# Eight phases of routed FFN with a moving-average attention: state adds on VectorE in the last phase, its last job in halves, gathers spread, attention batches moved forward, weight loads ahead of broadcasts on SyncE's queue

## The reference, cut to what matters

```python
xn = _layernorm(x)
# branch 1: per feature a causal convolution whose kernel is a sum of two decaying
# exponentials (an exponential moving average), plus xn * omega, then silu
out = irfft(rfft(xt, n=2*S) * rfft(k, n=2*S))[..., :S]
attn = silu(transpose(out) + xn * omega)
# branch 2: four rounds of a mixture of 4 experts, two of them for each token
for r in range(4):
    vals, idx = top_k(flat @ Wg[r] + bg[r], 2)
    cw = sum(one_hot(idx, 4) * softmax(vals)[..., None], axis=1)
    hmid = gelu(einsum('nh,ehf->enf', flat, W1) + b1[:, None, :])   # 128 -> 512
    y = einsum('enf,efh->enh', hmid, W2) + b2[:, None, :]           # 512 -> 128
    cur = cur + einsum('ne,enh->nh', cw, y)
x = x + attn + cur
```

## Time and profile before

| | |
|---|---|
| median of 3 runs | 706.83 us (705.14 to 710.83) |
| the profiled execution | 702.66 us |
| its span, first to last instruction | 700.8 us |
| mean granted TensorE clock | 0.961 |
| busy share of TensorE, its weight loads, VectorE, ScalarE, GpSimd | 88%, 73%, 68%, 74%, 59% |
| DMA, mean over the span | 208 GB/s |

### The profile page before, as it was taken

How to read it: one execution, slowest core, us unless ns; L and a number is a source line. 1 busy time by engine, 2 the same in 40 slices (tenths; PEclk the granted TensorE clock), 3 DMA queues, 4 the chain that set the end, 5 groups by cost and what they waited for, 6 DMA issues and landing times.

```text
span 700.8 us, 11414 instructions
## 1 busy us (share of the span) xinstructions
PE 616.5 (88%) x3289; PEld 508.3 (73%) x3289; DVE 473.7 (68%) x1049; ACT 515.9 (74%) x979; POOL 412.4 (59%) x432
## 2 busy tenths in 40 slices
PE   7667999999998998999989989998999898888580
PEld 6455877888787887888778877887788776677360
DVE  4963786688864885578656876587758875795350
ACT  4668778898786877788877877886788686777550
POOL 5658438552874375536843584438568785855664
PEclk9999999999999998999999999999899999999995
DMA  8011012646886587667975689568767798658510
GB/s 240 10 55 48 15 55 87 212 165 219 310 256 254 204 304 250 224 227 253 329 268 198 250 282 283 222 218 289 238 241 251 270 307 271 237 197 305 191 60 30
DMA packets 85898, 145.92 MB, mean 208 GB/s; under 512 B 21911, under 2 KB 49486, under 8 KB 85838
## 3 DMA queue, kind: packets, MB, share of 16 engines
q1 hardware_dynamic: 79540, 133.06, 54.8%
q0 software_dynamic: 5824, 11.87, 5.3%
q10 hardware_dynamic: 474, 0.28, 0.1%
HBM read 37.42 MB, written 12.09 MB: 71 GB/s over the span
## 4 chain that ended last, share of the span: by engine, by line
PE 50%; DVE 12%; POOL 10%; issue 9%; DMA 8%; ACT 5%; SPq 3%; another core or an unknown queue 1%; POOLq 1%; DVEq 1%; ACTq 0%
PE z L1383 8%; PE y L1399 8%; PE y L1401 7%; PE z L1385 7%; PE y L1400 7%; PE z L1384 7%; PE spare L1308 4%; POOL sorted_rows L754 4%; DVE h_lo L1216 3%; DMA w_job<-w_all 3%; POOL state L740 3%; DMA sorted_rows<-rows,position_i 3%; ACT z L889 2%; ACT h_hi L892 2%; PE misc L1330 2%
## 5 line engine op out<-in xcount | busy, mean ns | idle before, releaser
L1216 DVE TENSOR_TENSOR h_lo<-z,h_hi 128x512 fp32r<-128x512 f32 (+1 forms) x428 | 251.6, 597 | 132.6 <-ACT h_hi L892 99.1
L889 ACT ACTIVATE z<-z,b_job 128x512 f32<-128x512 f32 (+1 forms) x364 | 212.2, 583 | 102.9 <-PE z L1385 76.5
L892 ACT CAST h_hi<-z 128x512 fp32r<-128x512 f32 (+1 forms) x428 | 221.4, 517 | 13.5
L740 POOL TENSOR_TENSOR state<-state,weighted 128x512 f32<-128x512 f32 (+1 forms) x103 | 115.6, 1122 | 130.0 <-DVE weighted L1163 128.1
L1399 PE MATMUL y<-h_hi,w_job 128*128 128x512 f32 (+1 forms) x364 | 134.7, 370 | 22.6 <-DVE h_lo L1216 13.8
L1383 PE MATMUL z<-cur_hi,w_job 128*128 128x512 f32 (+1 forms) x364 | 139.3, 383 | 13.4 <-DMA w_job<-w_all 10.3
L754 POOL DMA_INDIRECT sorted_rows<-rows,position_i x112 | 118.2, 1055 | 32.6 <-issue 22.4
L1400 PE MATMUL y<-h_lo,w_job 128*128 128x512 f32 (+1 forms) x364 | 130.1, 357 | 0.0
L1401 PE MATMUL y<-h_hi,w_job 128*128 128x512 f32 (+1 forms) x364 | 129.9, 357 | 0.0
L1384 PE MATMUL z<-cur_lo,w_job 128*128 128x512 f32 (+1 forms) x364 | 129.8, 357 | 0.0
L1385 PE MATMUL z<-cur_hi,w_job 128*128 128x512 f32 (+1 forms) x364 | 129.4, 356 | 0.0
(11 more groups left out here) (164 smaller groups left out, 791.9 us busy)
## 6 DMA issues: line engine op xcount, KB each, us to landing
w_job<-w_all SPq DMA_DIRECT2D x182, 512.0 KB
gate_bc<-gate_rows SPq DMA_DIRECT2D x72, 256.0 KB
rows<-sorted_rows SPq DMA_DIRECT2D x28, 266.0 KB, 3.7
gate_bc<-gate_rows SPq DMA_DIRECT2D x35, 128.0 KB
out_dram<-x_tok SPq DMA_DIRECT2D x8, 256.0 KB, 5.5
sorted_rows<-rows,position_i POOLq DMA_INDIRECT x112
b_job<-b_all SPq DMA_DIRECT2D x91, 2.5 KB
rows<-in_L_ffn_W_dram SPq DMA_DIRECT2D x4, 256.0 KB, 7.5
```

The lines of the kernel that those rows point to most:

```text
L740: pool.tensor_tensor(state[job.g][:, cols_at], before, weighted[:, j % TR, 0:job.n], ALU.add).then_inc(added, 1)
L889: nc.scalar.activation(zs, zs, ACT.Gelu_apprx_tanh, bias=bias).then_inc(gelu_done, 1)
L892: nc.scalar.copy(h_hi[:, s % ZR, 0:job.n], zs).then_inc(hi_act, 1)
L1216: dve.tensor_tensor(h_lo[:, s % ZR, 0:job.n], zs, hs.bitcast(F32), ALU.subtract).then_inc(lo_done, 1)
```

## The change

**1. State adds of the last phase on VectorE.** `add_last(j)` stands right behind `combine(j)` on VectorE and replaces GpSimd's `add(j)` in phase 7. It counts up a semaphore of its own, `added_last`, on which the transpositions of that phase wait.

**2. The last job in halves.** F7 of phase 7 becomes H0 and H1 of 256 tokens with the same expert, weights being loaded for each. The transposition, addition and finish of the last block fall in two halves, called "Q", of two tiles each.

**3. Gathers and step numbers.** The gathers of phase 7 move from the steps 23 to 40 to the steps 6 to 37, those of phase 6 one or two steps ahead; several P steps of both phases move by up to 6.

**4. Attention.** EMA_PHASE changes from (1, 2, 3, 4, 5, 6, 7, 7) to (1, 1, 2, 2, 3, 4, 5, 6): the phases 1 and 2 work two batches each (the second at the steps 0 to 14), phase 7 none.

**5. SyncE's queue.** For a job it was W1, W2, bias of the same job, gate broadcast of the job before. Now it is W1, W2, and then bias and gate broadcast of the job behind it. W1 of a phase's first job is issued before `load_sorted` waits. `b_job` has 6 slots. Each of the four DMAs reads the table itself, so there are four TENSOR_LOADs for a job instead of two.

**6. Small moves.** P split 49 to 48, jobs 31 to 30, two scatters one step later.

```diff
-LAST_JOBS = "F0 F1 F2 F3 X0 X1 X2 X3 X4 F4 F5 F6 F7".split()
+LAST_JOBS = "F0 F1 F2 F3 X0 X1 X2 X3 X4 F4 F5 F6 H0 H1".split()
...
 SORTED = {
-    "P": (42, 44, 51, 53), "P copy": (46, 48, 53, 57), "P split": (44, 46, 49, 55),
+    "P": (42, 44, 51, 53), "P copy": (46, 48, 53, 57), "P split": (44, 46, 48, 55),
...
-    "places": (17, 18), "pairs": (22, 22), "order": 22, "pick": 27, "jobs": 31, "table": 35,
-    "scatter": (19, 20, 20, 20, 21, 23, 24, 24, 25, 27, 31, 33, 35, 35, 40, 42), "load": 45}
+    "places": (17, 18), "pairs": (22, 22), "order": 22, "pick": 27, "jobs": 30, "table": 35,
+    "scatter": (19, 20, 20, 20, 21, 23, 24, 24, 25, 27, 31, 33, 35, 36, 41, 42), "ema 2": (0, 1, 2, 3, 4, 6),
+    "ema tanh 2": 6, "A 2": 10, "A add 2": 14}
...
 LAST_PHASE = {
-    "P": (40, 41, 49, 58), "P add": (43, 44, 51, 61), "finish": (47, 45, 52, 63),
-    "ema": ((-3, 1, 2, 3, 4, 7), (9, 11, 12, 14, 15, 19)), "ema tanh": (5, 19), "A": (6, 19), "A add": (8, 22),
-    "idents": 26, "gather": (23, 25, 26, 27, 28, 28, 28, 30, 35, 35, 35, 36, 38, 38, 39, 40)}
+    "P": (38, 41, 47), "P add": (41, 43, 50), "finish": (41, 46, 53), "idents": 4,
+    "gather": (6, 9, 11, 11, 12, 12, 16, 17, 19, 22, 24, 26, 30, 31, 33, 37), "Q": (56, 56), "Q add": (57, 58),
+    "Q finish": (57, 58)}
 BEFORE_LAST = {
-    "P add": (43, 46, 53, 57), "finish": (48, 50, 54, 58), "idents": -1,
-    "gather": (1, 1, 2, 2, 3, 3, 4, 4, 6, 6, 6, 6, 7, 7, 11, 11)}
-EMA_PHASE = (1, 2, 3, 4, 5, 6, LAST, LAST)
+    "P add": (43, 46, 51, 53), "finish": (48, 51, 54, 57), "idents": -3,
+    "gather": (-1, 1, 2, 2, 3, 3, 3, 4, 4, 4, 4, 5, 8, 9, 11, 12)}
+EMA_PHASE = (1, 1, 2, 2, 3, 4, 5, 6)
...
-            for j in range(NJ + 1):
-                if DENSE <= j < NJ:
-                    job_weights(j)
-                if j > 0:
-                    job = JOBS[j - 1]
-                    if job.kind == "D" and job.e == 0:
+            for j, job in enumerate(JOBS):
+                if job.kind == "D":
+                    if job.e == 0:
                         gates_out(("G", 0, job.b))
-                    if job.kind == "F" and job.i == 0:
-                        gates_out(("G", job.p, 0))
+                    broadcast_gate(j)
+                    continue
+                last_of_phase = j + 1 == NJ or JOBS[j + 1].p > job.p
...
+                if job.turn == 0:
+                    sp.wait_ge(table_ready, 3 * job.p)
+                    job_bias(j)
+                job_w1(j)
+                if job.turn == 0:
+                    load_sorted(job.p)
+                job_w2(j)
+                if not last_of_phase:
+                    job_bias(j + 1)
+                if job.turn == 1:
+                    gates_out(("G", job.p, 0))
                     broadcast_gate(j - 1)
-                for p in SORT_GATE:
-                    if j == LOAD_AT[p] // FC + 1:
-                        load_sorted(p)
+                    broadcast_gate(j)
+                if job.turn > 0 and not last_of_phase:
+                    broadcast_gate(j + 1)
                 for b in range(B):
-                    if j == T_AT["A", b] // FC + 3:
+                    if j == ADD_AT["A", b] // FC + 3:
                         store_x(b)
...
+            def add_last(j):
+
+                job = JOBS[j]
+                if job.kind == "X":
+                    if job.i == 0:
+                        dve.wait_ge(table_ready, 3 * LAST)
+                    dve.reg_load(half_at, table_i[LAST % 2][0:1, 13 + job.i:14 + job.i])
+                    cols_at = bass.ds(dve.snap(half_at, min_val=0, max_val=GT - HALF), HALF)
+                else:
+                    cols_at = job_cols(job)
+                dve.wait_ge(combined, j + 1)
+                wait(dve, added_last, j - FIRST[LAST])
+                dve.tensor_tensor(state[1][:, cols_at], state[1][:, cols_at], weighted[:, j % TR, 0:job.n],
+                                  ALU.add).then_inc(added_last, 1)
```

More of the change, by code:

```diff
@@ L31 @@
 WR = 3
+BR = 6
 GR = 4
@@ L66, in job_list @@
             for turn, name in enumerate(LAST_JOBS if p == LAST else SORTED_JOBS):
-                full, i = name[0] == "F", int(name[1])
-                jobs.append(Job(p, g, name[0], i, i // 2 if full else None, None, BLK if full else HALF, turn))
+                kind, i = name[0], int(name[1])
+                b = {"F": i // 2, "X": None, "H": NB - 1}[kind]
+                jobs.append(Job(p, g, kind, i, b, None, BLK if kind == "F" else HALF, turn))
     return jobs, first
@@ L86, in block_done, with last_half_done, add_on_dve @@
     return 1 + max(j for j, job in enumerate(JOBS) if job.p == p and (job.kind == "X" or job.b == b))
+def last_half_done(half):
+    done = [j for j, job in enumerate(JOBS) if job.p == LAST and (job.kind == "X" or job.b == NB - 1)]
+    return 1 + max(j for j in done if JOBS[j].kind != "H" or JOBS[j].i == half) - FIRST[LAST]
+def add_on_dve(j):
+    return JOBS[j].p == LAST
 def hi_on_dve(s):
@@ L452, in wait, with job_cols @@
                 eng.wait_ge(s, value)
+        def job_cols(job):
+            first = job.b * BLK + (job.i * HALF if job.kind == "H" else 0)
+            return slice(first, first + job.n)
         def block_cols(b):
@@ L566, in broadcast_gate @@
                     start = from_table(job.p, 23 + job.i, ZERO_GATE - BLK)
+                elif job.kind == "H":
+                    start = from_table(job.p, 23 + 2 * NB - 1, ZERO_GATE - BLK) + job.i * HALF
                 else:
@@ L774, in _ @@
                 for j in range(max(s // FC - 3, 0), s // FC + 1):
-                    if combine_at(j) + 1 == s:
+                    if combine_at(j) + 1 == s and not add_on_dve(j):
                         add(j)
@@ L798, in _ @@
                             gather(p, t)
-                    for b in range(NB):
-                        if FINISH_AT[p, b] == s:
-                            finish(p, b)
-            add(NJ - 1)
-            for b in range(NB):
-                if FINISH_AT[LAST, b] >= STEPS:
-                    finish(LAST, b)
+                for name, when in FINISH_AT.items():
+                    if when == s:
+                        finish(name)
+            for name, when in FINISH_AT.items():
+                if when >= STEPS:
+                    finish(name)
             pool.wait_ge(out_done, 16 * B * TILES)
@@ L885, in _ @@
                     if c == 0 and job.kind != "D":
-                        act.wait_ge(job_b_in[slot(job)], 16 * uses(j))
-                    bias = b_all[:, job.e, c:c + 1] if job.kind == "D" else b_job[:, slot(job), c:c + 1]
+                        act.wait_ge(job_b_in[b_slot(j)], 16 * b_uses(j))
+                    bias = b_all[:, job.e, c:c + 1] if job.kind == "D" else b_job[:, b_slot(j), c:c + 1]
                     act.wait_ge(z_full, s + 1)
@@ L1154, in combine @@
                 job = JOBS[j]
-                b2_col = b_all[:, job.e, FC:FC + 1] if job.kind == "D" else b_job[:, slot(job), FC:FC + 1]
+                b2_col = b_all[:, job.e, FC:FC + 1] if job.kind == "D" else b_job[:, b_slot(j), FC:FC + 1]
                 if j == 0:
@@ L1261, in _ @@
                     if when == s:
-                        add_attention(name[1]) if name[0] == "A" else add_rows(name[1], name[2])
+                        add_attention(name[1]) if name[0] == "A" else add_rows(name)
             combine(NJ - 1)
-            for b in range(NB):
-                if ADD_AT["P", LAST, b] >= STEPS:
-                    add_rows(LAST, b)
+            add_last(NJ - 1)
+            for name, when in ADD_AT.items():
+                if when >= STEPS:
+                    add_rows(name)
         @block.tensor
@@ L1284, in to_spare @@
                     src = [rows[g][:, b * TILES + t, 0:H] for t in range(TILES)]
+                elif name[0] == "Q":
+                    half = name[2]
+                    pe.wait_ge(added_last, last_half_done(half))
+                    src = [state[1][:, (NB - 1) * BLK + half * HALF + t * P:(NB - 1) * BLK + half * HALF + (t + 1) * P]
+                           for t in range(TILES // 2)]
                 elif name[0] == "P":
                     g, b = where(name)
-                    pe.wait_ge(added, block_done(name[1], b))
+                    if name[1] == LAST:
+                        pe.wait_ge(added_last, block_done(LAST, b) - FIRST[LAST])
+                    else:
+                        pe.wait_ge(added, block_done(name[1], b))
                     src = [state[g][:, b * BLK + t * P:b * BLK + (t + 1) * P] for t in range(TILES)]
@@ L1380, in up @@
                 hi, lo = w1(job, c)
-                here = bass.ds(extra_cols[job.i], HALF) if job.kind == "X" else block_cols(job.b)
+                here = bass.ds(extra_cols[job.i], HALF) if job.kind == "X" else job_cols(job)
                 dst = z[:, s % ZR, 0:job.n]
```

90 lines of the change are left out of this document (57 added, 33 removed).

## The result

| | before | after |
|---|---|---|
| median of the runs made with the forecast's result | 705.99 us (702.49 to 710.83) | 717.83 us (715.71 to 721.81) |
| ratio, 95% interval | | 1.018 [1.013, 1.023] |
| span of the profiled execution | 700.8 us | 717.8 us |

The account below looks back on a forecast made before the run. TensorE, busiest in every phase, was taken as the bound, with gains only from its stops, lost clock and the tail. -10.8 + 6.0 - 8.5 - 5.7 = -19.0 us gave 688 us, range 670 to 702.

Parts of the forecast that it names:

- the reads hide in this back-pressure: Run of halves: two more table reads a job hide behind SyncE's held-up DMA issues, costing nothing.
- My first rival: SyncE's table reads not hidden in X0 to X4 and F4: 0.78 us a job, 29 us in all, 717 us; chance 0.07.
- W1's place ahead of `load_sorted`: First matmuls of a phase: F0's weights come sooner, saving 2.1 us in phase 1 and 1.9 in phase 3.
- SyncE's order: SyncE's queue: earlier first W1 and earlier gate rows together gain 10.8 us, ends 5.5 and 16.
- The gate rows that were to come earlier: Mid-phase at F4's combine: earlier gate broadcasts may end VectorE's unnamed wait; half credited, 3.0 us in phase 5, 2.3 in phase 2.
- Attention: Two batches cost +5 us in phase 1 and +1 in phase 2; stops gone from phase 7 save 2.0.
- Phase 7 and tail: Phase 7 gains 8.5 us from fewer stops; the tail gains 5.7 from VectorE's add and fewer finishes after the last y.
- The adds on VectorE at nothing: Phase 7: 14 state adds, some 8 us, cost nothing since VectorE loses two attention batches of 12.0 us.
- The rest: Phase 6 gathers and jobs a step ahead, scatters a step later: nothing beside the 2.2 us floor.
- the meeting of the earlier trace: VectorE scan meeting a GpSimd tensor operation took 3.93 us instead of 1.21; a few such meetings are in attention's +5.
- The sum: All parts: -10.8 + 6.0 - 8.5 - 5.7 = -19.0 us.

Follow-up runs that it names:

- a2_after: The kernel after, unaltered, run again on the quiet chip beside three variants: 694.74 us, 1.005 of before.
- a2_reads: The kernel after with two table reads for a job instead of four, on the quiet chip: 680.52 us, 0.983 of before.
- a_top: The kernel after with phase 1's load_sorted ahead of the table wait and two table reads a job, some made early: 673.24 us, 0.972 of before.
- b_pre: The kernel before with attention moved and the table reads of X0 to X4 and F4 made ahead during F0 to F2: 692.45 us, 0.983 of before.
- a_best: The kernel after with phase 7's adds on GpSimd, two table reads a job (some early), phase 1's load_sorted ahead of the table wait: 674.95 us, 0.981 of before.
- a_best_o: The same as a_best but with SyncE's order of before, load_sorted at its old place: 675.43 us, 0.980 of before.
- a_order: The kernel after with SyncE's order of before, keeping four table reads and six bias slots: 713.5 us, 1.019 of before.
- b_attn: The kernel before with the attention batches moved as in the change, plus the later store_x: 691.22 us, 0.989 of before.
- b_attn2: The kernel before with the attention batches moved alone, run again in another group: 680.17 us, 0.984 of before.
- a_paced: The kernel after with two table reads a job and phase 7's gathers waiting for VectorE to reach their steps: 702.3 us, 0.997 of before.
- a_small: The kernel after with two table reads a job; X jobs of phases 2 to 7 load 128 of 1024 weight columns: 701.9 us, 0.997 of before.

## Why the prediction was wrong, step by step

**The step that failed: "so I take it that the reads hide in this back-pressure: nothing."** They don't. On one chip the two reads cost 14.2 us beside a kernel of 680.5, and put into the kernel before they alone made it 2.2% slower [1.3%, 3.0%]. SyncE's pace from X2 to F6 went from 4.47 to 5.01 us, and at the closest from 4.10 to 4.92. My first rival had the right mechanism, and a chance of 0.07. Its 0.78 us a job is met only where the queue runs closest; with the mean of 0.54 its own sum gives 7 x (6 x 0.54 - 0.6) = 18 us instead of 29, and the runs have 14.2, since a phase loses 1.7 to 3.0 us (a2_after against a2_reads), not 4.1. That its 717 us is nearly the 717.8 us measured is luck: 14.2 of the reads, 6.6 of `load_sorted` and some 9 of the first chip happen to add up to its 29. The reason that I gave for back-pressure, DMA issues that stretch from 0.5 to 0.9 us with DMA engines near full, was true of some rows only (the mean DMA share from 626 to 641 was 0.76), and it said nothing of the register work between them. It was right for the first two reads: taking those out of the run of halves gained nothing that a_top or b_pre shows. The Trainium skill ("DMA: Bandwidth & Descriptors", "Latency and other measured facts") gives a floor of about 600 ns for a `tensor_load`, which would have made it 56 us, an estimate. The runs have 0.41 us for an added read with its register instructions at the closest and 0.27 in the mean, so the measurement decides against that figure.

**The step that I didn't make: load_sorted.** The forecast credited W1's place ahead of `load_sorted` and didn't ask what `load_sorted` itself now stands behind. In phase 0 it is the wait for phase 1's table; the rows came 7.4 us later (135.49 for 128.08), and 6.6 us of time hung on it.

**SyncE's order: forecast -10.8, measured about 0** (a_best against a_best_o, 0.5 us, give or take some 7 by their intervals; a_order points the same way). The waits at the first matmuls of phases 2 and 4 did go: F7 of phases 1 and 3 takes 6.0 us instead of 8.3 and 8.1. The gate rows that were to come earlier didn't matter, since no wait for them was the cause of the earlier trace rows: in the trace of before VectorE passes the gates' semaphore at 485.83 without waiting, and then waits for `y_full` (with `added`, raised at 480.90) until 489.35. `y_full` is raised at 489.31, although the matmul that raises it is recorded as ended at 486.09. In phase 2 it is the same, with 263.63 for a matmul recorded as ended at 261.92. I had half of this in the sum (3.0 and 2.3 us) for gate rows that it never hung on.

**Attention: forecast +6 in phases 1 and 2 and -2.0 in phase 7; measured -12 in all.** The size in phases 1 and 2 was too high: the first four jobs of both take 2.7 us more in b_attn and in b_attn2 than in the profile of before. Where the rest of the gain lies isn't shown, since the profile of before is of a chip with unnamed waits. In b_attn2 phase 7 is 10 us shorter than in it (F4 and F5 take 6.6 and 6.8 us for 8.6 and 16.1, and VectorE is busy 41 us of the phase instead of 54), the gathers no longer wait for the stored rows of the last batches (5.91 us before the first of them, at 638.41), and they begin 38.9 us into the phase instead of 40.8. But in b_attn, on a chip with such waits, phase 7 is as long as before (82.0 us), and phases 2, 4 and 5 are 3 us shorter each, although phase 2 got a batch more and the other two kept one. So the gain of 12 us is shown, on two chips with and without such waits (0.989 and 0.984), and its cause is open.

**Phase 7 and tail: forecast -8.5 and -5.7.** The tail was right: 20.5 to 15.1. The adds on VectorE at nothing were nearly right for phase 7 (72.8 us with them, 74.2 without), and 4.4 us of the tail's gain are theirs (15.2 and 19.6). The unbroken row of gathers that they leave cost nothing on the chip without unnamed waits. What phase 7 gained in all can't be read off, for want of a profile of before on such a chip.

**The rest: forecast nothing, measured 1.8 us.** The first four jobs of phase 6 take 28.2 to 28.3 us in the kernel before and its four variants, and 30.0 to 30.1 in the kernel after and its variants, on every chip. F2 takes 9.2 us for 6.4. In the trace after a small operation of VectorE meets an add and a split of GpSimd, which come together behind five gathers in a row, and ends when they do (VectorE, then GpSimd twice); TensorE then waits 1.58 us for the `h_lo` behind it:

```profile
551.80 3.07 DVE L1081 TENSOR_TENSOR below<-lg,top 128x64 f32<-128x64 f32 x1
...
552.25 1.30 POOL L792 TENSOR_TENSOR state<-state,weighted 128x512 f32<-128x512 f32 x1
553.50 1.27 POOL L772 TENSOR_TENSOR cur_lo<-state,cur_hi 128x512 fp32r<-128x512 f32 x1
```

In the trace of before the same operation takes 0.22 us (at 536.96). It takes 3.1 us in all variants of the kernel after but a_paced, where the operation ahead of it meets the two and takes 3.30 us for 0.43. It is the meeting of the earlier trace rows again, at a place that the forecast put at nothing.

**The sum.** By runs of one chip, the kernel after without its two faults is some 0.972: -19.4 us. Forecast was -19.0. That the parts counted on came to their sum is luck in part: the order was 10.8 too high and the attention some 16 too low. What was not counted, 14.2 + 6.6 us, ate it up: -19.0 + 20.8 = +1.8 us, and the quiet chip has +2.9. On the first chip it was +11.8, and these last 9 us came with the waits without a name.

**The waits without a name.** The kernel before takes 14 us more on the first chip than on the quiet one (706.0 and 691.8 us), the kernel after 23 (717.8 and 694.7), 16.6 of them in phase 7: 91.1 against 74.5. In the traces the sum of these waits (VectorE's and ScalarE's marked "remote") is 14.5 us before and 31.8 after on the first chip, and nothing in a2_after, where the same gathers run in the same unbroken row. So the row of gathers alone doesn't stop the other engines. Whether it makes the waits longer on a chip that has them stays open: there phase 7 was 80.7 us with the gathers held to their steps and 89.2 without (a_paced, a_small, which differ in the weights too). What the waits are stays open as well. They are not DMA bandwidth: a_small, with an eighth of the bytes, has more of them, and from 642 to 662 in the trace after the DMA engines are busy for 0.43. They are no wait that the records name, and SyncE's own register instructions (MOVE), 0.03 us elsewhere, take up to 0.70 us in that stretch, 0.36 in the median.

## What to carry to other kernels

An engine that only issues DMAs has a pace like any other. The first reads in its queue can be hidden and the next ones not: here two a job cost nothing that could be measured, and four cost 14 us. Reading a value once for a job and keeping it in a register took that back; reading it earlier still added nothing. When an instruction is moved in a queue, list what it now stands behind as well as what it is now ahead of. A step number spreads nothing on an engine that never waits; and a comparison of variants needs the kernel before and the changed kernel on the same chip, with a profile of both.

## What the runs showed of the hardware that was not expected

Two chips can differ in kind: the kernel before took 706 and 692 us on two of them, and the trace from the first has waits of VectorE and ScalarE for semaphores whose matmuls are recorded as ended 1.8 to 7.4 us earlier (14.5 us of waiting in all; in the trace after up to 15.5 us earlier, 31.8 us in all). On the quiet chip every wait of over 1.5 us for z ends within 0.1 us of the recorded end of its matmul (a2_after). A table read with its register instructions lengthens SyncE's period by 0.41 us where the queue runs closest, and by 0.27 in the mean of the run of halves, while a read alone is recorded at 0.24 to 0.27 us at best. Of VectorE and GpSimd either can be the one held. A scan of VectorE took 3.93 us for 1.21 and an operation on 64 columns 3.07 for 0.22, each until two operations of GpSimd behind one another had ended; in b_attn2, with the scan begun 0.16 us ahead, it was GpSimd's operation that took 2.14 us for 1.29.
